# A transformer block on one core: the tile of shifted columns moves to the end of the SBUF layout

## What is computed

```python
h = _layernorm(x) * (1 + ca) + sa
x = x + ga * ssm(h)          # ug = h W_in; dt, b from u; a scan over the tokens; y*silu(gate) + h*D; W_out
h = _layernorm(x) * (1 + cb) + sb
# channel mixing: xr, xk mix h with h of the token before
xr = mu_r * h + (1.0 - mu_r) * h_prev
xk = mu_k * h + (1.0 - mu_k) * h_prev
out = sigmoid(xr W_r) * (square(relu(xk W_k)) W_v)
x = x + gb * out
```

## Time and profile before

| | |
|---|---|
| median of 3 runs | 350.69 us (350.53 to 350.70) |
| the profiled execution's own time | 350.26 us |
| its span in the profile | 348.5 us |
| PE busy | 339.0 us, 97% of the span |
| DVE, ACT, POOL busy | 305.1, 294.4, 274.3 us |
| TensorE clock granted | full in all 40 slices |

### The profile page before, as it was taken

The page is one execution under the profiler, slowest core; times in us unless marked ns, Lnnn a source line. Parts: engine busy times, 40 slices in busy tenths (PEclk is TensorE's granted clock), DMA queues, the critical chain, the costliest instruction groups (busy, mean ns, idle before and its releaser), DMA issues.

```text
span 348.5 us, 5204 instructions
## 1 busy us (share of the span) xinstructions
PE 339.0 (97%) x1576; PEld 265.6 (76%) x1576; DVE 305.1 (88%) x463; ACT 294.4 (84%) x396; POOL 274.3 (79%) x273
## 2 busy tenths in 40 slices
PE   7999989899999999999999999999999999999995
PEld 4666667688888888888887888888888888887764
DVE  3889779999999999999999899999999989777846
ACT  4676787989898998989898998989899998888484
POOL 2241849989899998989899898989899896966742
PEclk9999999999999999999999999999999999999999
DMA  8950531051522506151331605151230501010013
GB/s 284 407 209 27 154 121 63 1 186 55 177 67 67 176 1 191 53 183 61 124 117 45 200 2 181 62 181 62 77 104 3 181 3 60 0 63 0 0 61 122
DMA packets 18556, 36.00 MB, mean 103 GB/s; under 512 B 4960, under 2 KB 5728, under 8 KB 18400
## 3 DMA queue, kind: packets, MB, share of 16 engines
q1 hardware_dynamic: 17808, 35.19, 29.8%
q10 hardware_dynamic: 720, 0.48, 0.4%
HBM read 27.22 MB, written 8.44 MB: 102 GB/s over the span
## 4 chain that ended last, share of the span: by engine, by line
PE 81%; DVE 7%; issue 4%; ACT 4%; POOL 2%; DMA 1%; SPq 0%; DVEq 0%; POOLq 0%; ACTq 0%
PE slot L292 67%; PE slot L385 4%; PE slot L299 3%; PE slot L536 2%; PE slot L527 2%; PE slot L526 2%; DMA w_in<-weights_in 1%; ACT prev L662 1%; DVE xn L919 1%; DVE xn L930 1%; DVE h L925 1%; POOL rstd L1166 1%; PE slot L393 1%; PE slot L332 0%; PE slot L306 0%
## 5 line engine op out<-in xcount | busy, mean ns | idle before, releaser
L1156 POOL TENSOR_TENSOR k_lo<-k_act,k_hi 128x512 fp32r<-128x512 f32 x30 | 51.2, 1727 | 4.6 <-ACT k_act L864 4.6
L662 ACT ACTIVATE prev<-slot,mod,mix_prev 128x512 f32<-128x512 f32 x64 | 46.5, 786 | 1.0 <-PE slot L592 0.7
L1156 POOL TENSOR_TENSOR xk_lo<-xk,xk_hi 128x512 fp32r<-128x512 f32 x30 | 38.4, 1296 | 8.1 <-ACT xk_hi L700 8.1
L292 PE MATMUL slot<-h_hi,wf_hi 128*128 128x512 f32 x120 | 43.8, 405 | 0.8 <-DVE z L994 0.8
L292 PE MATMUL slot<-h_hi,wf_lo 128*128 128x512 f32 x120 | 42.3, 393 | 0.0
L1156 POOL TENSOR_TENSOR xr_lo<-xr,xr_hi 128x512 fp32r<-128x512 f32 x32 | 41.9, 1311 | 0.3 <-ACT xr_hi L706 0.3
L1212 POOL TENSOR_TENSOR h_lo<-h,h_hi 128x512 fp32r<-128x512 f32 x28 | 36.3, 1299 | 2.4 <-ACT h_hi L681 2.4
L1266 POOL TENSOR_TENSOR z_lo<-z,z_hi 128x512 fp32r<-128x512 f32 x26 | 33.2, 1298 | 4.4 <-ACT z_hi L850 4.4
L292 PE MATMUL slot<-h_lo,wf_hi 128*128 128x512 f32 x120 | 34.9, 395 | 0.0
L964 DVE SCALAR_TENSOR_TENSOR xk<-slot,mix_new,prev 128x512 f32<-128x512 f32 x32 | 23.8, 747 | 8.0 <-issue 5.6
L930 DVE TENSOR_SCALAR xn<-slot,stats,rstd 128x256 f32<-128x256 f32 x62 | 29.2, 532 | 0.0
(11 more groups left out here) (161 smaller groups left out, 983.9 us busy)
## 6 DMA issues: line engine op xcount, KB each, us to landing
x_ch<-x_ch_in SPq DMA_DIRECT2D x16, 512.0 KB, 4.5
x_tok<-x_tok_in SPq DMA_DIRECT2D x15, 512.0 KB, 5.8
x_out<-wmod SPq DMA_DIRECT2D x15, 512.0 KB, 3.3
spread_rows<-rows_spread SPq DMA_DIRECT2D x13, 512.0 KB, 3.8
wmod<-wmod_in SPq DMA_DIRECT2D x1, 1024.0 KB, 8.6
w_in<-weights_in SPq DMA_DIRECT2D x1, 1024.0 KB, 11.3
w_in<-weights_in SPq DMA_DIRECT2D x1, 512.0 KB, 4.6
wmod<-wmod_in SPq DMA_DIRECT2D x1, 512.0 KB, 5.5
```

The costliest lines, as they stand in the source:

```text
L292: ins = nc.tensor.matmul(out, w[:, c, at + d * P:at + (d + 1) * P], x[:, c, :], start=first, stop=last)
L662: return nc.scalar.activation(prev[:, mix, i, 1:T + 1], ps_n[:, i, :], ACT.Identity, bias=mod_at(SHIFT2 + i, k), scale=mix_prev[:, mix, i, ...
L1156: nc.gpsimd.tensor_tensor(lo, x, hi.bitcast(F32), ALU.subtract).then_inc(done, 1)
```

## The change

One line moves: `prev` is allocated behind `r_gate`, as the last tile. No instruction is added, removed or moved; each engine's program is the same list of instructions with the same waits, and only addresses differ.

```diff
         z_lo = sb("z_lo", [P, CH, T], F32R)
-        prev = sb("prev", [P, 2, CH, T + 1])
         xk = sb("xk", [P, CH, T])
         xk_hi = sb("xk_hi", [P, CH, T], F32R)
         xk_lo = sb("xk_lo", [P, CH, T], F32R)
...
         k_lo = sb("k_lo", [P, CH, T], F32R)
         r_gate = sb("r_gate", [P, CH, T])
+        prev = sb("prev", [P, 2, CH, T + 1])
```

## The result

The changed kernel takes 348.3 us in the median of 22 runs (347.08 to 351.46), the kernel before, measured beside it, 351.06 us (22 runs). The ratio is 0.9911, with a 95% interval from 0.9891 to 0.9932: faster by 0.9%. The forecast was 348.0 us, 2.7 us less than the 350.69 us known then. The profiled execution took 347.91 us with a span of 346.1 us. Long executions are those in which the mean granted TensorE clock was lower: the 12 of the 22 at 0.998 of full speed or more took 347.08 to 348.35 us, the two at 0.990 took 350.67 and 351.46 us.

A forecast was written before the change was run, and what follows sets the result against it. TensorE's product rate was taken as the bound. Eleven steps (2.1 us), two later steps (0.5) and the tail (0.1) give 2.7 us off the 348.5 us span; 345.8 + 1.76 + 0.43 = 348.0 us, range 346.8 to 349.8.

The forecast's parts named there:

- The better level: Split products streaming tiles that begin at a multiple of 128 bytes: 226.5 ns each once settled.
- B: Second stretch of 26 products in a middle step, between transposes: 6.03 us to become 5.93, 0.10 less.
- C: Third stretch, a middle step's last 26 products: 6.00 us to become 5.93, its 0.07 lost to a later load.
- The other level: Split products streaming tiles not at a multiple of 128 bytes: 233.3 ns each, to vanish after the change.
- The rule that the gap is a matter of columns alone: Rival, 10%: product spacing depends on columns, with no term for the address; no effect, time stays at 350.7 us.
- The boundary: Between two steps, the first `xk_hi` load waits on VectorE's last `xk`; cuts PE's 0.30 us a step to 0.19.
- The pair: First two products of a step, the first being `xk_hi`: to take about 0.70 us instead of 0.63.
- A: First stretch, 20 products in a middle step: 4.66 us to become 4.53, 0.13 less, minus 0.04 for starting anew.
- This load had no reserve left: First `xk_hi` product's load, already idle 0.15 us before the change, would come later as the last stretch shortens by 0.07 us.
- The pause at every boundary: Rival, 15%: every step boundary shows the longer wait seen at 186.27 us; gain 1.0 to 1.8 us, 349.3 us.
- PE gets the whole gain: Rival, 10%: the load comes early enough, so all 13 steps give 0.30 us; about 4.1 us, 346.6 us.
- The slower rival: Rival, 5%: changing the streamed tile costs by itself, only the last stretch shortens, boundary loads come late; about 351.9 us.

The follow-up runs named there:

- experiment 2: Changed kernel with 32 unused bytes in front of `xk`, `prev` staying last: ratio 1.0017.
- experiment 5: Changed kernel with unused bytes in front of `h`, weights as before: 32 bytes, ratio 1.0025; 256 bytes, ratio 0.9899.
- experiment 6: Changed kernel with `k_hi` and `k_lo` moved behind `r_gate` and 32 unused bytes, so only `k` products are slow: ratio 0.9898.
- Experiment 1: Kernel before, with `prev` in its old place and 96 unused bytes behind it: 350.27 us, ratio 0.9983.
- experiment 4: Changed kernel with everything 128 bytes further, ratio 0.9918; everything 32 further, 0.9898; only the weights 32 further, 1.0024.
- experiment 7: VectorE's two statistics instructions taken apart: on the changed kernel 347.16 us, ratio 0.9883; on the layout of before, ratio 1.0000.
- experiment 8: Changed kernel with `x_tok`, `x_ch`, `x1`, `xn2` moved to the identity's place modulo 256, `xn1` 128 bytes from it: ratio 0.9890.

## Why the prediction came out right, and where it did not

**The rate of the streams** was read rightly. The better level and the slow start behind transposes are what the changed kernel shows: 226.3 ns in the 8 products behind 121.30 us (226.6 unrounded; forecast 226.5), and B at 5.91 us against the 5.93 of the sum. C was forecast at 5.93 us and is that, though 0.03 of it is a pause. The other level, 233.3 ns, comes back where streams stand at distance 32 (experiments 2, 5 and 6).

**The cause was put wrongly.** The step of the forecast that failed is the reading that a streamed tile's own start address, as a multiple of 128, sets the rate. Experiment 1 has all streams at such multiples and no gain that can be told; in experiment 4, with everything further by 32, none is at one, and the whole gain is there. What counts is the distance from the weight tiles modulo 256. The trace before could not tell the two, since the weights stood still at 128 modulo 256 and the good tiles did as well; I never wrote the weights' addresses beside those of the streams. The size survived by luck: the change happens to set this distance to 0. Had `prev` been padded in its place, the forecast of 348.0 us would have missed by over 2 us.

**The rule that the gap is a matter of columns alone**, the rival with 10%, is out: the same 1576 instructions of PE take 2.7 us less. The 216 ns that the Trainium skill ("TensorE: Matmul & The Clock Gate", "Back-to-back issue gap") gives for an isolated matmul of 512 columns are reached at no distance that ran; 226.3 ns is the best.

**The boundary** was right in place and in the total. The sum had 0.19 us a step, a step of 19.64 or 19.65 us; it is 19.64. The pair takes 0.70 us as read from the paused boundary of the earlier trace rows. Of the forecast gain of PE alone, 0.30 us, 0.11 was said to be lost there; experiment 7 gives back 0.12. Experiment 6 shows the reverse: time in C is free. The split between the stretches was not as forecast. A was to gain 0.13 less 0.04 and C's 0.07 was to be lost; measured between first products, A gains nothing and C its whole 0.07. "This load had no reserve left" holds for the second product, which starts 0.34 us behind the load before and after. The first product had 0.07 to 0.08 us of reserve, since it can follow its load by 0.03 us and followed it by 0.11. Counted from the second pair, A gains 0.07 and B 0.12, and these two make the 0.19 of a step; forecast were 0.09 and 0.10. I had the first product start on time; PE pauses for 0.03 us before it.

**The steps summed up.** Eleven steps gave 2.55 us, forecast 2.1; the difference is mainly the first boundaries, where PE waits in both kernels and at 86.98 us the late load of the earlier trace rows is gone. The end gave 0.7 us, forecast 0.6. The prologue was put at zero; with loads deciding when it ends, and the first boundary lying anywhere from 66.9 to 68.4 us over all profiles, these runs can't show a gain there of the 0.3 us that it might have had.

**The pause at every boundary** (15%) did not come: one boundary of the changed kernel, at 185.82 us, shows the longer form with 0.41 us of idle time, near the 186.27 us of before. In it the load comes 0.34 us behind the last `xk` instead of 0.18. Its cause stays open. It is missing in both runs with the split statistics, where `xk` is earlier, but also in experiments 1 and 8 and in most others, so that says little.

**PE gets the whole gain** (10%) is what experiment 7 reaches by another edit: 19.51 us a step and a span 4.0 us shorter than before, where this rival had 4.1. Its terms as written, 3.9, 0.1 and 0.3, add up to 4.3.

**The slower rival** (5%) held that a change of the streamed tile costs by itself, so that A and B stay as they are. The changed kernel refutes it: B, in which the streamed tile changes over and over, fell by 0.12 us, to 227.3 ns a product. That a layout can make this kernel slower is shown by experiment 5 and by the moved weights, some 0.25% each, with intervals that begin just above 1.

**The other engines** were put at zero and are: ScalarE's rounding of `xk` takes 627 ns and that of `z`, a tile that did not move, 627 ns.

## What to carry to other kernels

For split products, write down the start of each streamed tile and of its weights modulo 256 bytes, and make them equal; one odd-sized tile in the middle of the layout shifts all that stand behind it. Where one engine is busy for 97% of the span, compare the start-to-start time of its equal instructions by tile: a few ns between groups, times a thousand instructions, is a percent. And before counting such a gain, look for the load that has no reserve left, since the next chain takes over right there and may need an edit of its own.

## What the runs showed of the hardware that I had not expected

- Split (`float32r`) products of 512 columns settle at 226.6 ns from start to start when stream and weights begin at the same place modulo 256 bytes, and take 228.5 ns with 64 bytes between them, 232.4 with 128 and 233.4 with 32; weights 32 bytes ahead instead of behind give 396 ns in the duration by tile, as slow as the other way. No other distances ran. Since moving the weights alone is enough, the read of the next weights and that of the stream seem to get in each other's way; that is argued, not shown. Plain fp32 products take 602 ns at distance 32 and at 0.
- A fast stream needs some products to settle behind transposes or a gap (231.7 ns over six of them). Behind slow products it has to settle again: 0.93 us for four `h` products in experiment 6, 0.91 in the changed kernel.
- With five waits in front of it, the first load comes 0.18 us behind VectorE's last `xk`, in both kernels (up to 0.34 us at a few boundaries, for a cause not found); the product follows 0.03 us behind the load if PE is waiting, and the second product not before 0.34 us behind the load.
